# Transposing the row maxima of an attention batch: one matrix and four copies for four matrices and two copies

## The chip, the cores and the metric

One core of a Trainium2 chip runs the whole kernel. The metric is device time in microseconds (us) from start to end of one execution. The kernel before takes 259.82 us (median of three runs, 259.51 to 259.97).

## The reference, cut to what matters

Eight sequences of 128 tokens with 256 features go through a gated cross-attention (8 key heads of 8 features, 32 query heads, four of them to a key head) and then a gated mixture of 16 experts, of which each token uses two. The part around the change is the softmax of the attention:

```
q = (layernorm(x) @ Wq.T + bq);  k = ctx @ Wk.T + bk;  v = ctx @ Wv.T + bv
scores = einsum('bgrqd,bgkd->bgrqk', q, k) / sqrt(8)
scores = where(causal_mask, -inf, scores);  scores = where(padding_mask, -inf, scores)
w   = softmax(scores, axis=-1)
out = einsum('bgrqk,bgkd->bgrqd', w, v)          # then @ Wo.T + bo, gate, residual, experts
```

## The kernel before, in words

The kernel is written instruction by instruction: five programs, one for each engine, meet at semaphores, and the order on each engine is fixed by tables of slot numbers.

**What a batch does.** A batch is one of the eight sequences. Its scores are made twice by TensorE. `scores_q` computes them with queries on the partitions (128 queries by 4 key heads x 128 keys), in eight products (4 values of r, 2 halves hf of the heads); VectorE's `row_max` (L849) takes the negated maximum over the keys of each, so that `mneg` [128, R=4, G=8] holds 32 maxima for each query. `scores_k` computes the scores again, transposed, with keys on the partitions, in eight products (one for each key head g), which ScalarE's `Exp` (L668) turns into `pT`. The maximum must be subtracted per query, and queries then lie in the free dimension, so the subtraction is part of the product: the moving operand `q4` [128, 2, R, tokens] carries the three-part queries in its partitions 0 to 95 and the negated maxima in its partitions 96 to 111 (8 rows of high parts, 8 of low parts, `KR` = 3*QR + 2*G = 112), and the stationary operand `kz` has ones there for its head.

**The job MT** brings the maxima from `mneg` into these partitions. `max_parts` (L859 and L861, VectorE) writes their high and low parts into `mt`, at columns 96 to 111 of each of four matrices of 128 x 112, one for each r; the other columns are zero from a memset at the start (L470, GpSimd). TensorE transposes the four matrices (L1046), side by side into one PSUM bank, where the 16 wanted rows lie at partitions 96 to 111, 512 columns wide. ScalarE copies them to `q4`, once for each half of the heads (L588, L589: the two copies read the same 16 x 512 values), and the second copy raises `mt_ok`.

**The order of the work.** The main loop has 82 slots. In slot s < 64 TensorE issues `scores_k(s)` (L989: the mask product, listed in the trace as bank<-ident_b,cmask, then bank<-q,kz), then `scores_q` of 12 or so products ahead (bank<-kz,q, then bank<-cmask,ident_b), in slots with s % 8 == 5 and 0 the products with the values (bank<-pT,vz), and then the jobs of the slot. MT of batch b stands in slot 8b - 3, MT of batch 0 ahead of the loop. ScalarE takes a job's result one slot later, before the `Exp` of that slot: the copies of MT, b stand ahead of `Exp(8b - 2)`. `scores_k(n)` waits for `p_done` n - 1, that is for `Exp(n - 2)`, whose bank it writes; and for the first head of a batch, `scores_k(8b)`, also for `mt_ok` of its batch. So `scores_k(8b)` is the first product of TensorE that waits for what stands behind MT on ScalarE. Other jobs are TO, AT, WO, YT (output of attention: transposes, the product with Wo, the next transpose), SC, SN, CT and CB (router and expert weights). After slot 63 come the experts, all products of TensorE with VectorE and ScalarE behind it.

Of the kernel before, what the change touches and what calls it, by code (L numbers as in the profile page):

```python
# [92 lines left out]
def build(nc, x, ctx_in, m_qk, m_pad, g_x, g_f, Wq, bq, Wk, bk, Wv, bv, Wo, bo, Rw, Gw, Uw, Dw, consts, pick, out):  # L93
    es = ExitStack()
    with es:
# [54 lines left out]
        rstd = sb("rstd", [P, NB])  # L150
        nmr = sb("nmr", [P, NB])
        mneg = sb("mneg", [P, R, G])
        mt = sb("mt", [P, R, KR], F32R)
        pT = sb("pT", [P, 2, G // 2, R * L])
        o_sb = sb("o_sb", [P, R * L])
        rden = sb("rden", [P, R, G])
# [184 lines left out]
        def toks(t):  # L341
            return slice(t * L, (t + 1) * L)
# [214 lines left out]
        def _(sc):  # L557
# [4 lines left out]
            def high(j):  # L562

                sc.wait_ge(job_done, jn[j] + 1)
                ps, k = jbank(j), j[0]
                if k == "wkv":
                    ins = nc.scalar.copy(wkv[0], ps[:, 0:NKW].rearrange("p (c n) -> p c n", c=DC))
                elif k == "wq":
                    for c in range(DC):
                        ins = nc.scalar.copy(wq[0][:, c].rearrange("p (r g d) -> p r g d", r=R, g=G),  # L570
                                             ps[:, c * D:(c + 1) * D].rearrange("p (g r d) -> p r g d", g=G, r=R))
                elif k == "wo":
                    ins = nc.scalar.copy(wo[0][:], ps[:].rearrange("p (c n) -> p c n", c=DC))
                elif k in ("c", "x"):
                    ins = nc.scalar.copy((cT if k == "c" else xT)[0][:, j[2], half(j[1])], ps[:])
                elif k == "kv":
                    for hf in range(2):
                        ins = nc.scalar.activation(k4[0:QR, hf, half(j[1])], ps[QR * hf:QR * (hf + 1), :],
                                                   ACT.Identity, bias=bias[QR * hf:QR * (hf + 1), 2 * R + hf:2 * R + hf + 1])
                        if hf == 0:  # L580
                            ins.then_inc(job_hi, 1)
                elif k == "q":
                    ins = nc.scalar.activation(qc_hi[1][:, j[2]], ps[:], ACT.Identity,
                                               bias=bias[:, 2 * R + 3 + j[2]:2 * R + 4 + j[2]])
                elif k == "MT":
                    rows = slice(3 * QR, KR)
                    src = ps[rows, :].rearrange("p (r q) -> p r q", r=R)
                    nc.scalar.copy(q4[rows, 0, :, toks(j[1])], src)  # L588
                    nc.scalar.copy(q4[rows, 1, :, toks(j[1])], src).then_inc(mt_ok, 1)  # L589
                    return  # L590
                elif k == "AT":
                    if j[1]:
                        sc.wait_ge(job_done, jn["WO", j[1] - 1] + 1)
                    ins = nc.scalar.copy(aT[0][:], ps[:, 0:D].rearrange("p (c q) -> p c q", c=DC))
                elif k == "YT":
                    ins = nc.scalar.copy(xT[0][:, :, toks(j[1])], ps[:, 0:D].rearrange("p (c q) -> p c q", c=DC))
                ins.then_inc(job_hi, 1)
# [90 lines left out]
        def _(ve):  # L688
# [163 lines left out]
            def max_parts(b):  # L852

                ve.wait_ge(max_ok, G * (b + 1))
                if b:
                    ve.wait_ge(job_done, jn["MT", b - 1] + 1)
                else:
                    ve.wait_ge(pool_init, 3)
                own(nc.vector.tensor_copy(mt[:, :, 3 * QR:3 * QR + G], mneg[:]))  # L859
                settle()  # L860
                nc.vector.tensor_tensor(mt[:, :, 3 * QR + G:KR], mneg[:], mt[:, :, 3 * QR:3 * QR + G].bitcast(F32), ALU.subtract).then_inc(m_parts, 1)  # L861


            def best_two(h):
# [122 lines left out]
        def _(pe):  # L987
# [12 lines left out]
            def job(j):  # L1000
# [13 lines left out]
                elif k in ("wq", "wo"):  # L1014
                    src = wq_n if k == "wq" else wo_n
                    pe.wait_ge(d_wq if k == "wq" else d_wo, 16)
                    for c in range(DC):
                        for o in range(DC):
                            ins = nc.tensor.transpose(ps[:, c * D + o * P:c * D + (o + 1) * P],
                                                      src[:, o, c * P:(c + 1) * P], ident)  # L1020
                elif k in ("c", "x"):
                    _, h, c = j
                    if k == "c":
                        pe.wait_ge(d_ctx, 16 * (h + 1))
                    else:
                        pe.wait_ge(xn_ok, 1 + TPH * h)
                    src = c_sb if k == "c" else xn
                    for t in range(TPH):
                        ins = nc.tensor.transpose(ps[:, toks(t)], src[:, h * TPH + t, c * P:(c + 1) * P], ident)  # L1029
                elif k == "vn":  # L1030
                    pe.wait_ge(v_ok, j[1] + 1)
                    for b in range(TPH):
                        ins = nc.tensor.transpose(ps[:, b * 64:(b + 1) * 64], vT[64:128, toks(j[1] * TPH + b)],
                                                  ident[64:128, 64:128])
                elif k == "kv":
                    pe.wait_ge(*emptied(("c", j[1], 1)))
                    ins = three(ps[:], [lambda c, i=i: wkv[i][:, c] for i in range(2)],
                                [lambda c, i=i: cT[i][:, c, half(j[1])] for i in range(2)], DC)
                elif k == "q":
                    pe.wait_ge(*emptied(("x", j[1], 1)))  # L1040
                    ins = three(ps[:], [lambda c, i=i: wq[i][:, c, j[2] * P:(j[2] + 1) * P] for i in range(2)],
                                [lambda c, i=i: xT[i][:, c, half(j[1])] for i in range(2)], DC)
                elif k == "MT":
                    pe.wait_ge(m_parts, j[1] + 1)
                    for r in range(R):
                        ins = nc.tensor.transpose(ps[0:KR, r * L:(r + 1) * L], mt[:, r].bitcast(F32), ident)  # L1046
                elif k == "TO":
                    pe.wait_ge(o_ok, j[1] + 1)
                    for r in range(R):
                        ins = nc.tensor.transpose(ps[:, r * P:(r + 1) * P], o_sb[:, r * L:(r + 1) * L], ident)  # L1050
                elif k == "AT":
                    pe.wait_ge(*emptied(("TO", j[1])))
                    a = an[:].rearrange("p g r d -> p (g r d)")
                    for c in range(DC):
                        ins = nc.tensor.transpose(ps[:, c * L:(c + 1) * L], a[:, c * P:(c + 1) * P], ident)  # L1055
                elif k == "WO":
                    pe.wait_ge(*emptied(("AT", j[1])))
                    ins = three(ps[:, 0:D], [lambda c, i=i: aT[i][:, c] for i in range(2)],
                                [lambda c, i=i: wo[i][:, c] for i in range(2)], DC)
                elif k == "YT":  # L1060
                    pe.wait_ge(xn_ok, 1 + TPH + j[1] + 1)
                    for c in range(DC):
                        ins = nc.tensor.transpose(ps[:, c * L:(c + 1) * L], xn[:, j[1], c * P:(c + 1) * P], ident)  # L1063
                elif k == "SC":
                    pe.wait_ge(*emptied(("YT", (j[1] + 1) * TPH - 1)))
                    pe.wait_ge(rw_ok, 1)
                    ins = three(ps[:], [lambda c, i=i: rw[i][:, c] for i in range(2)],
                                [lambda c, i=i: xT[i][:, c, half(j[1])] for i in range(2)], DC)
                elif k == "SN":
                    pe.wait_ge(*emptied(("SC", j[1])))  # L1070
                    for t in range(TPH):
                        ins = nc.tensor.transpose(ps[:, t * E:(t + 1) * E], s16[0:E, toks(j[1] * TPH + t)], ident[0:E, 0:E])
                elif k == "CT":
                    pe.wait_ge(c2_ok, j[1] + 1)
                    for t in range(TPH):
                        ins = nc.tensor.transpose(ps[0:2 * E, toks(t)],
                                                  c2[:, j[1] * TPH + t].rearrange("p a e -> p (a e)").bitcast(F32), ident)
                elif k == "CB":
                    t, h = ORDER[j[1]]
                    pe.wait_ge(*emptied(("CT", h)))  # L1080
                    pe.wait_ge(pick_ok, 1)
                    ins = mm(ps[:], pick_r[:, t * P:(t + 1) * P], cwT[:, half(h)], True, True)
# [131 lines left out]
```

## Time and profile before

| | |
|---|---|
| median of three runs | 259.82 us |
| the profiled execution, its own time | 257.8 us |
| its span in the trace | 256.0 us |
| mean granted TensorE clock | 0.973 of full speed |
| TensorE busy with products | 228.1 us, 1243 instructions |
| VectorE busy | 174.8 us |
| ScalarE busy | 93.8 us |
| GpSimd busy | 98.3 us |

The first 19 us load and prepare, the attention's eight batches run to about 136 us, the experts from there to the end. PE is TensorE's products, PEld its weight loads, DVE VectorE, ACT ScalarE, POOL GpSimd. In the rows below a product's time is longer than its share of the engine, since products overlap; what one costs in a stream is read from the distance of the starts.

### The profile page before, as it was taken

The page shows a single profiled execution, that of the slowest core. Times are in us where ns is not written, and L with a number is a line of the kernel's source. Part 1 is how long each engine was busy: PE and PEld are TensorE (multiplying, and loading weights), DVE is VectorE, ACT ScalarE, POOL GpSimd, SP SyncE. Part 2 cuts the span into 40 slices and gives each one's busy share as a digit, 9 for nine tenths or more (in the row PEclk, how much of TensorE's full clock was granted, in tenths as well). Part 3 has the DMA queues.
Part 4 walks back from the last instruction along what each step waited for, and adds up shares of the span by engine and source line. Part 5 has one row for each costly group of instructions (what it writes and reads, how often), then busy time and mean ns, then how long its engine had stood idle before and what let it go on. Part 6 is the DMA issues. An engine that isn't in the chain of part 4 may idle for free.

```text
span 256.0 us, 3715 instructions
## 1 busy us (share of the span) xinstructions
PE 228.1 (89%) x1243; PEld 163.0 (64%) x1243; DVE 174.8 (68%) x358; ACT 93.8 (37%) x175; POOL 98.3 (38%) x131
## 2 busy tenths in 40 slices
PE   0679698999989999999588899799999999999993
PEld 0653364466545555555335787688888888888882
DVE  2659678658797677858921775698665766676565
ACT  2554248746656574747376221001010101011000
POOL 5355514400836193811711022229742563362000
PEclk9995589999999999999999999999999999999999
DMA  7571600007740002020020000003402220000004
GB/s 211 69 229 41 155 15 23 0 10 170 162 94 1 3 0 61 3 63 0 12 53 0 0 4 0 0 0 85 102 16 50 61 42 22 0 0 0 3 0 164
DMA packets 22418, 12.31 MB, mean 48 GB/s; under 512 B 14816, under 2 KB 21568, under 8 KB 22400
## 3 DMA queue, kind: packets, MB, share of 16 engines
q1 hardware_dynamic: 22096, 11.86, 19.4%
q10 hardware_dynamic: 304, 0.22, 0.4%
q8 instruction: 10, 0.16, 0.3%
q14 instruction: 8, 0.07, 0.1%
HBM read 7.91 MB, written 1.05 MB: 35 GB/s over the span
## 4 chain that ended last, share of the span: by engine, by line
PE 76%; DVE 13%; SPq 3%; DMA 3%; issue 2%; ACT 2%; DVEq 0%
PE bank L989 70%; DVE mneg L849 2%; DMA mqk_u<-in_mask_SxS_bc 2%; PE bank L1046 2%; PE bank L1050 2%; SPq L374 1%; PE bank L1029 1%; DVE x_sb L982 1%; DVE cb L895 1%; DMA q<-q 1%; DVE w L891 1%; PE bank L1055 1%; DVE xT L715 1%; DVE rw L953 1%; PE bank L1063 1%
## 5 line engine op out<-in xcount | busy, mean ns | idle before, releaser
L989 PE MATMUL bank<-xT,cT 128*128 128x512 f32 x288 | 70.5, 394 | 0.0
L989 PEld LDWEIGHTS bank<-xT,cT 128*128 128x128 f32 x288 | 53.7, 188 | 12.1 <-issue 0.8
L849 DVE TENSOR_REDUCE mneg<-bank 128x4 f32<-128x512 f32 x64 | 43.2, 685 | 13.8 <-PE bank L989 12.6
L668 ACT ACTIVATE pT<-bank 128x512 f32<-128x512 f32 x64 | 38.2, 599 | 23.6 <-PE bank L989 22.7
L655 ACT ACTIVATE pT<-bank 128x512 f32<-128x512 f32 x24 | 14.3, 597 | 81.1 <-PE bank L989 81.1
L989 PEld LDWEIGHTS bank<-w_d,q 128*128 128x128 f32 x288 | 37.4, 190 | 2.8 <-issue 1.3
L989 PE MATMUL bank<-w_d,q 128*128 128x256 f32 x288 | 38.3, 282 | 0.8 <-DVE q L927 0.8
L989 PE MATMUL bank<-q,kz 112*128 112x512 f32 x64 | 38.2, 598 | 0.0
L989 PE MATMUL bank<-kz,q 96*128 96x512 f32 x64 | 28.3, 452 | 3.3 <-DMA q<-q 1.9
L912 DVE TENSOR_TENSOR pT<-pT,bank 128x512 f32<-128x512 f32 x24 | 16.4, 683 | 18.5 <-PE bank L989 18.5
L921 DVE TENSOR_TENSOR pT<-pT,bank 128x512 f32<-128x512 f32 x24 | 16.5, 686 | 16.3 <-PE bank L989 16.0
L989 PE MATMUL bank<-cmask,ident_b 128*128 128x512 bf16 x64 | 26.4, 412 | 0.0
L989 PE MATMUL bank<-ident_b,cmask 128*128 128x512 bf16 x64 | 24.9, 389 | 1.2 <-ACT q L589 1.2
L453 POOL TENSOR_TENSOR vare<-mv,cst 128x1 f32<-128x1 f32 (+1 forms) x10 | 1.9, 194 | 60.7 <-DVE mv L703 53.4
L927 DVE TENSOR_TENSOR q<-pT,q 128x512 fp32r<-128x512 f32 x24 | 22.4, 933 | 0.8
L526 POOL TENSOR_TENSOR w_d<-padf,zero 128x256 fp32r<-128x256 f32 x12 | 7.4, 614 | 36.8 <-PE bank L989 36.5
L484 POOL TENSOR_TENSOR kz<-k,cst 112x512 fp32r<-112x512 f32 x16 | 16.3, 1043 | 11.1 <-DVE k L718 6.3
L523 POOL TENSOR_TENSOR cT<-c_sb,cT 128x512 fp32r<-128x512 f32 x12 | 18.1, 1509 | 0.9
L989 PEld LDWEIGHTS bank<-cmask,ident_b 128*128 128x128 bf16 x64 | 6.5, 101 | 17.9 <-issue 17.7
L989 PE MATMUL bank<-pT,vz 128*32 128x512 f32 x128 | 17.0, 605 | 0.7 <-ACT pT L668 0.7
L989 PEld LDWEIGHTS bank<-kz,q 96*128 96x128 f32 x64 | 13.0, 203 | 7.1 <-DVE mneg L849 3.3
L522 POOL TENSOR_TENSOR cT<-c_sb,zero 128x512 fp32r<-128x512 f32 x12 | 14.0, 1164 | 0.0
(131 smaller groups left out, 291.9 us busy)
## 6 DMA issues: line engine op xcount, KB each, us to landing
padf<-in_L_ffn_down_w SPq DMA_DIRECT2D x12, 128.0 KB, 2.3
c_sb<-in_ctx SPq DMA_DIRECT2D x2, 512.0 KB, 6.5
q<-cT SPq DMA_DIRECT2D x8, 128.0 KB, 2.7
out<-x_sb SPq DMA_DIRECT2D x4, 256.0 KB, 2.4
q<-xn SPq DMA_DIRECT2D x8, 96.0 KB, 2.2
c_sb<-in_L_ffn_gate_w SPq DMA_DIRECT2D x8, 96.0 KB, 2.1
c_sb<-in_L_ffn_up_w SPq DMA_DIRECT2D x8, 96.0 KB, 2.1
x_sb<-in_x SPq DMA_DIRECT2D x2, 256.0 KB, 3.6
```

Of the source, the lines that this page charges most:

```text
L484: ins = pool.tensor_tensor(kz[0:KR, s, g], k4[0:KR, hf, toks(b)].bitcast(F32).unsqueeze(1).to_broadcast([KR, GH, L]), cst[0:KR, C_G + GH * ...
L522: step(pool.tensor_tensor(w_gu[0][:, s], gu, zero[:].unsqueeze(2).unsqueeze(3).to_broadcast([P, 2, DC, P]), ALU.add))
L523: pool.tensor_tensor(w_gu[1][:, s], gu, w_gu[0][:, s].bitcast(F32), ALU.subtract).then_inc(w_ok, 1)
L526: step(pool.tensor_tensor(w_d[0][:, s], raw_d[:, s], zero[:].to_broadcast([P, D]), ALU.add))
L655: nc.scalar.activation(act_g[:, n % 2], bank[0][:], ACT.Silu).then_inc(a_ok, 1)
L668: nc.scalar.activation(pT[:, i // 4, i % 4, :], bank[2 + s % 2][:], ACT.Exp, scale=SCALE).then_inc(p_done, 1)
L849: nc.vector.tensor_reduce(mneg[:, r, 4 * hf:4 * hf + 4], bank[SQ_BANK[n % 3]][:].rearrange("p (g k) -> p g k", g=4), X, ALU.max, negate=Tr ...
L912: nc.vector.tensor_tensor(h_su[:, n % UL], act_g[:, n % 2], bank[1][:], ALU.mult).then_inc(u_free, 1)
L921: nc.vector.tensor_tensor(h_all, h_su[:, n % UL], jbank(j)[:], ALU.mult).then_inc(job_lo, 1)
L927: nc.vector.tensor_tensor(hl[:, n % 2], h_all, hh[:, n % 2].bitcast(F32), ALU.subtract).then_inc(h_ok, 1)
L989: return nc.tensor.matmul(dst, a, b, start=start, stop=stop, skip_group_check=True)
L1046: ins = nc.tensor.transpose(ps[0:KR, r * L:(r + 1) * L], mt[:, r].bitcast(F32), ident)
```

## The change

`mt` becomes one matrix of 128 x 128: for each r a block of 32 columns, of which the first 16 hold the high and low parts and the rest zeros. One transpose puts them all into the first 128 columns of the bank, the maxima of r at partitions 32r to 32r + 15. ScalarE then makes four copies, one for each r, each out of another quadrant of 32 partitions (32r), 16 partitions by 2 x 128 elements: the source is read twice (a stride of zero over the two halves of the heads), and the destination is partitions 96 to 111 of `q4`, both halves, that r. The last raises `mt_ok`. VectorE's two instructions write the same 32 values of a partition, at other columns.

```diff
-        mt = sb("mt", [P, R, KR], F32R)
+        mt = sb("mt", [P, R, P // R], F32R)
...
                 elif k == "MT":
-                    rows = slice(3 * QR, KR)
-                    src = ps[rows, :].rearrange("p (r q) -> p r q", r=R)
-                    nc.scalar.copy(q4[rows, 0, :, toks(j[1])], src)
-                    nc.scalar.copy(q4[rows, 1, :, toks(j[1])], src).then_inc(mt_ok, 1)
+                    for r in range(R):
+                        src = ps[r * P // R:r * P // R + 2 * G, 0:L].unsqueeze(1).to_broadcast([2 * G, 2, L])
+                        ins = nc.scalar.copy(q4[3 * QR:KR, :, r, toks(j[1])], src)
+                    ins.then_inc(mt_ok, 1)
                     return
...
-                own(nc.vector.tensor_copy(mt[:, :, 3 * QR:3 * QR + G], mneg[:]))
+                own(nc.vector.tensor_copy(mt[:, :, 0:G], mneg[:]))
                 settle()
-                nc.vector.tensor_tensor(mt[:, :, 3 * QR + G:KR], mneg[:], mt[:, :, 3 * QR:3 * QR + G].bitcast(F32), ALU.subtract).then_inc(m_parts, 1)
+                nc.vector.tensor_tensor(mt[:, :, G:2 * G], mneg[:], mt[:, :, 0:G].bitcast(F32), ALU.subtract).then_inc(m_parts, 1)
...
                 elif k == "MT":
                     pe.wait_ge(m_parts, j[1] + 1)
-                    for r in range(R):
-                        ins = nc.tensor.transpose(ps[0:KR, r * L:(r + 1) * L], mt[:, r].bitcast(F32), ident)
+                    ins = nc.tensor.transpose(ps[:, 0:L], mt[:].rearrange("p r m -> p (r m)").bitcast(F32), ident)
```

On TensorE, around MT of batch 2 (bank<-cst,mt is the transpose of `mt`, bank<-cst,an that of the job AT ahead of it; lines behind L1045 move up by one):

```order
 L989 MATMUL bank<-cmask,ident_b 128x512
 L989 MATMUL bank<-pT,vz 32x512 x4
-L1055 MATMUL bank<-cst,an 128x128 x2
-L1046 MATMUL bank<-cst,mt 112x128 x4
+L1054 MATMUL bank<-cst,an 128x128 x2
+L1045 MATMUL bank<-cst,mt 128x128
 L989 MATMUL bank<-ident_b,cmask 128x512
 L989 MATMUL bank<-q,kz 128x512
```

Four transposes have become one, in the same place; nothing else on TensorE moves, in this batch or in the others.

On ScalarE, at the same batch (q<-bank are the copies of the maxima, pT<-bank the exponentials, aT<-bank the job AT):

```order
 L668 ACTIVATE pT<-bank 128x512
 L594 CAST aT<-bank 128x256
-L588 CAST q<-bank 16x4x128
-L589 CAST q<-bank 16x4x128
+L588 CAST q<-bank 16x2x128 x4
 L668 ACTIVATE pT<-bank 128x512 x4
 L644 COPY o_sb<-bank 128x512
```

Two copies of 512 elements a partition have become four of 256, ahead of the same four exponentials.

## Rows read from the trace of the kernel before

**Rows 1.** The page: busy time, share of the span and instructions of each engine.
```profile
PE 228.1 (89%) x1243; PEld 163.0 (64%) x1243; DVE 174.8 (68%) x358; ACT 93.8 (37%) x175; POOL 98.3 (38%) x131
```

**Rows 2.** Windows: length, busy us (x) of PE, PEld, DVE, ACT, POOL, clock, DMA.
```profile
85.08:96.80 11.72, 11.72 (x71) 6.50 (x67) 8.25 (x16) 7.46 (x14) 7.47 (x11) 1.00 0.01 1
...
27.00:34.00 7.00, 4.76 (x17) 3.03 (x17) 3.60 (x10) 2.35 (x5) 4.61 (x5) 0.50 0.55 125
34.00:35.00 1.00, 1.00 (x8) 0.81 (x8) 0.91 (x2) 0.55 (x2) 0.00 (x0) 0.97 0.00 0
```

**Rows 3.** Timeline, batch 4: start, us, engine, line, operation, [idle before]; TensorE from MT on.
```profile
85.08 0.65 PE L1046 MATMUL bank<-cst,mt 128*112 128x128 f32 x4
85.57 0.38 PE L989 MATMUL bank<-ident_b,cmask 128*128 128x512 bf16 x1
...
88.13 0.38 PE L989 MATMUL bank<-ident_b,cmask 128*128 128x512 bf16 x1
```

**Rows 4.** Timeline, ScalarE, batch 4: the two copies, and the exponential behind them.
```profile
85.77 0.58 ACT L588 CAST q<-bank 16x512 fp32r<-16x512 f32 x1 [1.44 <-PE bank L1046]
...
86.86 0.60 ACT L668 ACTIVATE pT<-bank 128x512 f32<-128x512 f32 x1
```

**Rows 5.** The tile mt: TensorE's 32 transposes, ns least/median/most.
```profile
L1046 PE MATMUL bank<-cst,mt x32: 272/273/432, 28.1 to 122.5; 128*112 128x128 f32 x32
```

**Rows 6.** Timeline, TensorE: the two transposes of YT, and the product behind them.
```profile
81.74 0.38 PE L1063 MATMUL bank<-cst,xn 128*128 128x128 f32 x2
81.96 0.38 PE L989 MATMUL bank<-ident_b,cmask 128*128 128x512 bf16 x1
```

**Rows 7.** Timeline, batch 0: TensorE and ScalarE around the first MT.
```profile
28.09 1.07 PE L1046 MATMUL bank<-cst,mt 128*112 128x128 f32 x4 [1.31 <-DVE mt L861]
...
29.19 0.58 ACT L588 CAST q<-bank 16x512 fp32r<-16x512 f32 x1 [5.48 <-PE bank L1046]
29.68 0.57 ACT L589 CAST q<-bank 16x512 fp32r<-16x512 f32 x1
...
30.31 0.61 PE L989 MATMUL bank<-ident_b,cmask 128*128 128x512 bf16 x1 [1.15 <-ACT q L589]
```

**Rows 8.** Timeline, ScalarE: runs of two or eight instructions with nothing between them.
```profile
10.50 0.65 ACT L570 CAST w_t<-bank 128x256 fp32r<-128x256 f32 x2
...
15.89 3.06 ACT L610 ACTIVATE q<-bank,bias 32x128 fp32r<-32x128 f32 x8
...
39.15 1.39 ACT L578 ACTIVATE k<-bank,bias 32x512 fp32r<-32x512 f32 x2 [1.77 <-PE bank L989]
```

**Rows 9.** One line's instructions, L610: least, median and most ns.
```profile
L610 ACT ACTIVATE q<-bank,bias x8: 358/360/362, 15.9 to 18.6; 32x128 fp32r<-32x128 f32 x8
```

**Rows 10.** Timeline, batch 2: TensorE and ScalarE around MT.
```profile
60.18 0.60 PE L1046 MATMUL bank<-cst,mt 128*112 128x128 f32 x4
...
60.38 0.37 ACT L594 CAST aT<-bank 128x256 fp32r<-128x256 f32 x1 [1.20 <-PE bank L1055]
...
61.91 1.09 ACT L668 ACTIVATE pT<-bank 128x512 f32<-128x512 f32 x2
...
63.18 0.39 PE L989 MATMUL bank<-ident_b,cmask 128*128 128x512 bf16 x1
```

**Rows 11.** Timeline, batch 1: TensorE's MT and its `scores_k(8)`.
```profile
43.96 0.62 PE L1046 MATMUL bank<-cst,mt 128*112 128x128 f32 x4
...
47.16 0.38 PE L989 MATMUL bank<-ident_b,cmask 128*128 128x512 bf16 x1
```

**Rows 12.** Timeline, batch 7: MT, and TensorE's wait for the router's weights.
```profile
122.16 0.65 PE L1046 MATMUL bank<-cst,mt 128*112 128x128 f32 x4 [0.94 <-DVE xT L715]
...
126.76 0.60 PE L1076 MATMUL bank<-cst,c 128*32 128x128 f32 x4 [2.33 <-DVE c L901]
```

**Rows 13.** The chain of waits: the piece of VectorE that starts the way to it.
```profile
118.93 0.70 DVE mneg L849
```

**Rows 14.** Timeline, GpSimd: its first instruction behind the memsets of the start.
```profile
15.09 0.46 POOL L492 TENSOR_TENSOR cmask<-padf,mqk 128x128 bf16<-128x128 f32 x1 [6.55 <-DVE padf L836]
```

## The prediction
> **What bounds the kernel now.** I read the page first: TensorE is busy in 89% of the span, no other engine in more than 68% [rows 1]. An average hides stages, so I took one batch of the attention from one MT to the next by the view of windows [rows 2]: 11.72 us long, TensorE busy in all of them, VectorE in 8.25, ScalarE in 7.46, and the clock at full speed. There TensorE's stream of products is the bound, and what is taken out of it shortens the batch, as long as nobody else's wait fills the gap. The same view shows the granted clock at 0.50 from 27 to 34 us, the lower of the two levels (1.2 GHz), and at 0.97 from 34 to 35, nearly the upper (2.4 GHz). Then the timelines around each MT give what its transposes cost, when ScalarE's copies follow, and when TensorE next needs something that stands behind them.
>
> **TensorE, batches 1 to 6.** The products overlap, so the price is the distance of the starts. YT's two transposes start at 81.74 and the product behind them at 81.96: 0.22, or 0.11 each [rows 6]. MT's four take 0.49, from 85.08 to 85.57 [rows 3], a little over four times 0.11, since the first doesn't find its weights loaded; that part stays. Three fewer save 3 x 0.11 = 0.33 us in a batch, 6 x 0.33 = **1.98 us**. That each transpose now has 128 columns of weights and not 112 I cost at nothing: YT's have 128 already.
>
> **ScalarE's copies, their price.** A cast of 256 elements a partition takes 0.37 us [rows 10], one of 512 takes 0.58 [rows 4]. How closely can four follow? The two copies before start 0.49 apart though the first lasts 0.58: they overlap by 0.09 [rows 7]. The casts of L570 do as well: two in 0.65, so 0.65 - 0.37 = 0.28 apart [rows 8, 10]. But these pairs start in one and the same quadrant. L610 reads each of its eight instructions out of another quadrant than the one before (QR * i), and there 3.06 = 7 x 0.386 + 0.36: they start 0.386 apart and last 0.360 [rows 8, 9], with no overlap and a gap of 0.026. L578's two, from quadrants 0 and 1, take 1.39, again no overlap [rows 8]. The new copies are of that kind. So the interval is between 0.28 (overlap) and 0.60 (as long as the old ones, none); I take 0.37 + 0.026, about **0.39**, since L610 is the nearest row. The page "ScalarE: Activation LUTs" of the Trainium skill, section on what ACT_TABLE_LOAD costs, says that back-to-back ACTIVATEs overlap by about 93 ns, and makes no exception for quadrants. By that the copies would be 0.28 apart and the gain larger, the first rival below; the trace agrees where the quadrant stays, and disagrees at L610 and L578.
>
> **Does ScalarE make TensorE wait?** What stands behind the copies is `Exp(8b - 2)`, and `scores_k(8b)` waits for it and for `mt_ok`. In batch 4 the one transpose starts at 85.08 and lasts 0.27 [rows 3, 5]; before, the four ended at 85.73 and ScalarE started at 85.77 [rows 3, 4], 0.04 behind, so now it starts at 85.39. Four copies take 1.56, so the exponential starts at 86.95 (before 86.86) and ends 0.60 later, at 87.55. TensorE now comes to `scores_k(8b)` at 88.13 - 0.33 = 87.80 [rows 3]. A slack of 0.25 is left, about 0.2 with the semaphore: hidden, but narrowly; before it was 88.13 - 87.46 = 0.67. Batch 1: 43.96 + 0.31 + 1.56 + 0.60 = 46.43 against 47.16 - 0.33 = 46.83 [rows 11], hidden. Batches 3, 5 and 6 are built as batch 4. Batch 2 differs: ScalarE is at AT's cast from 60.38 to 60.75 and can only then start the copies, at 60.78; exponential at 62.34, end 62.94, and TensorE wants it at 63.18 - 0.33 = 62.85 [rows 10]. TensorE waits about 0.13, and a weight load of the mask may come uncovered: I take **0.2 us lost**, between 0 and 0.3.
>
> **Batch 0** stands ahead of the loop, at half clock, and all of it is on the path: DVE, four transposes, two copies, product [rows 7]. The transposes: 28.09 to 29.19 when ScalarE starts; one of them lasts 0.43 at this clock [rows 5], the longest of the 32, so ScalarE starts at 28.55, 0.64 earlier. The copies: 3 x 0.39 + 0.37 = 1.54 for 1.06, 0.48 longer. TensorE goes on 0.16 earlier. It then works at half speed until 34; if the clock rises at the same instant as before, half of that is lost again. I take **0.1**, between 0.08 and 0.16 (with overlap 0.49).
>
> **Batch 7**: nothing. MT at 122.16 is followed by a wait of 2.33 for the router's weights at 126.76 [rows 12], which VectorE makes in a chain that starts at 118.93 from a product of TensorE [rows 13]. The gains of the batches before move that start, this one's only lengthens the wait; the copies have that time too.
>
> **The rest.** GpSimd's memset of `mt` is shorter by 320 elements, and it idles 6.55 before its next work [rows 14]: nothing. VectorE's instructions keep their sizes, and at a stride of 32 elements instead of 112 I expect the same time; it idles 3.5 us of a batch [rows 2]. No DMA and no wait of another engine is moved; MT's bank comes free with `mt_ok`, two slots and more before the next job there.
>
> **Sum**: 1.98 - 0.2 + 0.1 + 0 = **1.9 us**. The profiled execution took 257.8 with a span of 256.0; it would take 255.9. It lies 2.0 below the median of the runs shown, a difference I can't place; the gain hangs on the attention's stretch at full clock, so I put it on the median: 259.8 - 1.9 = **257.9 us**.
>
> **Rivals.**
> 1. *The copies overlap in spite of the quadrants* (0.28 apart). Batch 2 doesn't wait, batch 0 gives 0.49 at the engine, about 0.35 at the end: 1.98 + 0.35 = 2.3, so 257.5. For it: a copy without a pointer operand is the simpler instruction, and L610 and L578 have one, in changing quadrants too. Against: nothing else distinguishes L610 from L570.
> 2. *Part of the gain is taken up on the way.* The slack of 0.2 in batches 3 to 6 is small. Copies 0.45 to 0.50 apart would make TensorE wait 0.05 to 0.25 in each of four batches and 0.4 to 0.6 in batch 2; or VectorE's maxima, which TensorE awaits in the early batches, don't shift with it. Gain about 1, 258.8.
> 3. *ScalarE becomes the bound behind each MT, and the kernel is slower.* The place is `scores_k(8b)`, the price the interval of the copies. At 0.60 the exponential of batch 4 ends at 85.39 + 2.40 + 0.60 = 88.39; TensorE waits 0.6 and loses 0.3 against before. Four such batches 1.2, batch 1 0.15, batch 2 0.64, batch 0 about 0.5: 2.5 slower, 262.3. It turns at about 0.52. For it: a source read twice through a stride of zero has no row of its own. Against: the elements written are counted in every row I have, and there are half as many.
> 4. *The clock rises later.* Before MT of batch 0 TensorE idles 1.31 and behind it 1.15 [rows 7]; now it does less and idles about 1.6 behind it, in the stretch at 0.50. Every us more at that level costs a busy engine half a us; 3.8 more would take all the gain, and the time would stay at 259.8. From 30.3 on TensorE is as busy as before, which speaks against it.
>
> That the change doesn't do what it says I exclude: both lists of instructions show one transpose and four casts at each of the eight places.
>
> **How the numbers follow.** A measurement of this kernel can tell 0.2%, 0.5 us, from no change. Forecast (gain 1.4 to 2.2) 0.55; rival 1 (2.2 to 2.9) 0.13; rival 2 (0.5 to 1.4) 0.17; rival 4 or another near zero 0.08; rival 3 0.07. Faster 0.85, same 0.08, slower 0.07. The range takes in the first three and the upper edge of the fourth: 256.9 to 259.3.
>
> **What would show it.** The copies' interval behind MT: 0.39 confirms the quadrants, 0.28 rival 1, over 0.45 rivals 2 or 3. MT to the next product 0.16 instead of 0.49. The window from MT to MT 11.4 instead of 11.72. ScalarE as releaser of `scores_k(16)`, once, with 0.1 to 0.2; the same at 24, 32, 40 and 48 would be rival 2. TensorE's start behind the first copies at 30.15, and the clock up at 34. The wait before CT 2.3 plus 0.3 at most. Wrong would be a batch that stays at 11.7.

## The result, and the profile after

The changed kernel takes 256.42 us (median of four, 256.26 to 258.50), the kernel before 259.89 in the same rounds; the ratio is 0.990, 95% interval 0.986 to 0.994. Twelve more executions gave 256.56, ratio 0.991 (0.988 to 0.994). So the changed kernel is faster, by about 1%, 1.5 to 3.8 us; the medians say 3.3 to 3.5, the ratio 2.4 to 2.6, the two profiled executions 257.8 - 256.26 = 1.5. Why these three differ is the larger part of what follows. Forecast was a gain of 1.9, in a range of times from 256.9 to 259.3, and the median of 256.42 lies 0.5 below that range.

The page of the profile after: busy time, instructions, and the clock in 40 slices.

```profile
PE 225.4 (89%) x1219; PEld 160.6 (63%) x1219; DVE 174.5 (69%) x358; ACT 97.0 (38%) x191; POOL 98.0 (39%) x131
...
PEclk9999589999999999999889999999999999999999
```

TensorE has 24 products fewer and 2.7 us less busy time, ScalarE 16 instructions and 3.2 us more [rows 1]. The clock row shows two dips, one near 30 us, which the first profile of before has too, and one near 126 us, which it doesn't have.

The windows of the profile after: batch 4 from MT to MT, and two stretches for the clock (the last three columns are granted clock, DMA share and GB/s).

```profile
83.52:94.91 11.39, 11.39 (x67) 6.20 (x64) 8.24 (x16) 7.83 (x16) 7.45 (x11) 1.00 0.00 0
126.00:131.00 5.00, 4.62 (x24) 2.07 (x17) 0.78 (x2) 2.82 (x6) 0.46 (x3) 0.71 0.19 49
32.00:36.00 4.00, 4.00 (x20) 2.54 (x18) 2.66 (x6) 2.27 (x4) 0.98 (x2) 0.84 0.11 23
```

The batch takes 11.39 for 11.72 [rows 2]: 0.33, as the sum had it, TensorE still busy in all of it. TensorE and ScalarE in this batch (start, us, engine and line, as in the rows of before):

```profile
83.52 0.33 PE L1045 MATMUL bank<-cst,mt 128*128 128x128 f32 x1
83.69 0.38 PE L989 MATMUL bank<-ident_b,cmask 128*128 128x512 bf16 x1
...
86.25 0.38 PE L989 MATMUL bank<-ident_b,cmask 128*128 128x512 bf16 x1
...
83.89 1.49 ACT L588 CAST q<-bank 16x256 fp32r<-16x256 f32 x4 [1.12 <-PE bank L1045]
85.41 1.17 ACT L668 ACTIVATE pT<-bank 128x512 f32<-128x512 f32 x2
```

MT takes 0.17 of TensorE's stream instead of 0.49 [rows 3]. The four copies take 1.49: at 0.364 each, (1.49 - 0.364) / 3 = 0.375 apart, no overlap. The exponential starts 1.89 behind MT (before 1.78 [rows 3, 4]) and ends at 85.41 + 0.60 = 86.01, 0.24 ahead of `scores_k(32)` at 86.25. Batch 2, where ScalarE is late:

```profile
59.29 0.27 PE L1045 MATMUL bank<-cst,mt 128*128 128x128 f32 x1
...
62.06 0.39 PE L989 MATMUL bank<-ident_b,cmask 128*128 128x512 bf16 x1
...
61.40 1.09 ACT L668 ACTIVATE pT<-bank 128x512 f32<-128x512 f32 x2
```

From MT to `scores_k(16)` it is 2.77, before 3.00 [rows 10]: 0.23 gained, 0.10 spent on the wait. But that 0.10 comes back before the batch is over. MT of batch 3 waits for VectorE in both kernels, 1.07 after and 1.19 before, and starts 72.21 - 59.29 = 12.92 behind MT of batch 2, before 73.45 - 60.18 = 13.27: the batch gains 0.35, as much as the others. The two MT of batch 3, after and then before:

```profile
72.21 0.33 PE L1045 MATMUL bank<-cst,mt 128*128 128x128 f32 x1 [1.07 <-DVE xT L715]
```

```profile
73.45 0.65 PE L1046 MATMUL bank<-cst,mt 128*112 128x128 f32 x4 [1.19 <-DVE xT L715]
```

Batch 0 and the wait for the router's weights:

```profile
27.80 0.45 PE L1045 MATMUL bank<-cst,mt 128*128 128x128 f32 x1 [1.59 <-DVE mt L861]
29.83 0.61 PE L989 MATMUL bank<-ident_b,cmask 128*128 128x512 bf16 x1 [1.58 <-ACT q L588]
...
124.21 0.60 PE L1075 MATMUL bank<-cst,c 128*32 128x128 f32 x4 [2.64 <-DVE c L901]
```

From MT to the next product 2.03 for 2.22 [rows 7]; the wait before CT 2.64 for 2.33 [rows 12]. In all, the profile after is 2.55 us ahead of the profile before when CT starts (124.21 for 126.76), and only 1.5 ahead at the end. Of the 2.55, 0.29 are there before MT of batch 0 starts (27.80 for 28.09), before the change has touched TensorE or ScalarE; such an offset stands between profiles of one program up to there too (27.68 and 28.03 in after_fill0 and after_fill2). The missing 1.0 us lies right behind CT, where the clock stands at 0.50.

### The profile page after: what moved, and what is told of

It reads as the page before. It is cut to its first block, busy times and chain, and to the rows that moved or that the text cites. A ratio compares the mean times of both kernels' runs of the same rounds, so it can differ in the third digit from the quotient of the medians.

```text
span 254.5 us, 3683 instructions
## 1 busy us (share of the span) xinstructions
PE 225.4 (89%) x1219; PEld 160.6 (63%) x1219; DVE 174.5 (69%) x358; ACT 97.0 (38%) x191; POOL 98.0 (39%) x131
## 4 chain that ended last, share of the span: by engine, by line
PE 79%; DVE 13%; DMA 3%; issue 2%; ACT 2%; ACTq 0%; DVEq 0%
PE bank L989 71%; DVE mneg L849 3%; PE bank L1029 2%; DMA wkv_n<-in_L_xattn_Wv 2%; PE bank L1049 2%; DVE x_sb L982 1%; DVE cb L895 1%; DMA q<-q 1%; PE bank L1045 1%; DVE w L891 1%; PE bank L1054 1%; ACT q L588 1%; DVE xT L715 1%; DVE rw L953 1%; PE bank L1062 1%
## 5 line engine op out<-in xcount | busy, mean ns | idle before, releaser
L989 PEld LDWEIGHTS bank<-w_d,q 128*128 128x128 f32 x288 | 37.4, 190 | 2.8 <-issue 1.3
L989 PE MATMUL bank<-q,kz 112*128 112x512 f32 x64 | 39.0, 611 | 0.0
L989 PE MATMUL bank<-kz,q 96*128 96x512 f32 x64 | 26.6, 425 | 4.8 <-DVE mneg L849 3.2
L989 PE MATMUL bank<-cmask,ident_b 128*128 128x512 bf16 x64 | 25.0, 391 | 0.0
L989 PE MATMUL bank<-pT,vz 128*32 128x512 f32 x128 | 17.7, 626 | 0.7 <-ACT pT L668 0.7
L989 PEld LDWEIGHTS bank<-kz,q 96*128 96x128 f32 x64 | 12.4, 194 | 8.5 <-DVE mneg L849 4.7
L588 ACT CAST q<-bank 16x256 fp32r<-16x256 f32 x32 | 11.6, 364 | 12.1 <-PE bank L1045 11.8
```

What stands on the lines that cost most here:

```text
L588: ins = nc.scalar.copy(q4[3 * QR:KR, :, r, toks(j[1])], src)
L989: return nc.tensor.matmul(dst, a, b, start=start, stop=stop, skip_group_check=True)
```

## The experiments

A table first, of all fourteen profiled executions, since each has pieces that can be set side by side. Times in us; "stretch" is from MT of batch 1 to CT of the first half, "behind" from there to CT of the second half, and "start" from the product behind MT of batch 0 to MT of batch 1, each from the chain of waits and the timeline of that profile. The clock is the granted one of two windows. The last four rows are of kernels with fillers or with CT moved, which come further down.

| kernel | time | start | stretch | behind | clock 32 to 36 | 126 to 131 |
|---|---|---|---|---|---|---|
| before, first profile | 257.80 | 13.65 | 82.80 | 36.40 | 0.74 | 1.00 |
| before_look_a | 259.87 | 14.04 | 82.90 | 37.84 | 0.63 | 0.66 |
| before_look_b | 257.54 | 13.44 | 82.84 | 36.40 | 0.81 | 1.00 |
| three_back | 258.40 | 13.61 | 82.71 | 36.39 | 0.66 | 1.00 |
| before_fill2 | 256.76 | 13.68 | 82.64 | 36.42 | 1.00 | 1.00 |
| changed, first profile | 256.26 | 13.55 | 80.83 | 37.42 | 0.84 | 0.71 |
| after_again | 256.07 | 14.40 | 80.81 | 36.34 | 0.59 | 1.00 |
| one_quadrant | 258.52 | 15.57 | 80.85 | 37.85 | 0.50 | 0.68 |
| after_fill2 | 255.23 | 13.59 | 80.72 | 36.35 | 1.00 | 1.00 |
| six_copies | 259.72 | 14.66 | 82.53 | 37.68 | 0.50 | 0.73 |
| before_fill0 | 260.32 | 15.33 | 82.88 | 37.61 | 0.69 | 0.81 |
| after_fill0 | 259.03 | 16.01 | 80.90 | 37.92 | 0.77 | 0.66 |
| ct_later | 253.57 | 13.51 | 80.91 | 34.74 | 0.85 | 1.00 |
| ct_later_fill0 | 254.13 | 13.68 | 80.89 | 34.68 | 1.00 | 1.00 |

The stretch is the same within 0.3 in all six profiles with four transposes, and within 0.2 in the seven with one transpose and four copies, 2.0 apart. Most of what varies between executions of a kernel is in the two other columns, and it goes roughly with the clock beside it: "behind" is 36.3 to 36.4 where the clock stays up and 37.4 to 37.9 where it falls, as long as CT is in its old slot. The windows are fixed, so a fall that reaches past one is shown in part only (both kernels with the first fillers).

### The changed kernel again

No edit.

> The changed kernel, unchanged, for more executions and the granted clock of each. Theory A (three transposes fewer in each of six batches, 0.33 us each, plus some tenths at batch 0; what else differs between executions is TensorE's clock, which falls at other places): MT to the next product 0.11 to 0.17, four copies 0.375 apart, 2.0 to 2.8 us faster than before in the median. Rival B (the gain of 3.5 us in the medians is all the change's): 3.3 to 3.6 faster again, and executions of the same clock as before's show it too.

Measured: 256.56 us median of 12 (255.58 to 258.92) beside 259.81 of before (257.61 to 260.53, 29 executions), ratio 0.991 (0.988 to 0.994). Copies 0.375 apart, MT 0.16 of the stream. By the medians it is rival B's 3.3. But the executions of both kernels fall into groups: of before, 6 of 29 lie under 258.5 and 22 over 259.3; of the changed kernel, 9 of 12 under 257.0 and 3 over 258.2. The lower groups are some 1.3 us apart, the upper ones 1.2; the median compares the upper group of the one with the lower of the other. So B's number came, but not by its reason; what the change is worth at the same clock, the pieces of the table and the fillers below tell. That the lower groups are 1.3 apart and not 2.0 fits the table: both profiles of the changed kernel are from its lower group, and each pays at one of the two places (37.42 behind CT in the first, 14.40 in the start in after_again), while before_look_b, from the lower group of before, pays at neither.

### Three transposes put back

```diff
-                    ins = nc.tensor.transpose(ps[:, 0:L], mt[:].rearrange("p r m -> p (r m)").bitcast(F32), ident)
+                    for r in range(R - 1, -1, -1):
+                        ins = nc.tensor.transpose(ps[:, r * L:(r + 1) * L], mt[:].rearrange("p r m -> p (r m)").bitcast(F32), ident)
```

> One part undone: TensorE transposes the one matrix four times (the first three into columns that nobody reads), ScalarE keeps its four copies. Theory A: six batches give back 0.33 us each and batch 0 about 0.3 to 0.6, so 2.3 to 2.6 slower than the changed kernel and about as slow as before or up to 0.5 us slower. Rival C (the gain comes from the later or shorter work of ScalarE or from GpSimd's shorter memset): stays within 0.5 us of the changed kernel.

Measured: 260.35 us median of 12 (258.40 to 261.46), 3.8 over the changed kernel, more than expected; ratio to before 1.004 (1.002 to 1.007). Profile beside profile it is 258.40 - 256.07 = 2.3, the expected size, 1.9 of it in the stretch (82.71 for 80.81); at batch 0 it is 2.66 from MT to the next product for 2.02, the 0.6 of the expectation's upper end. The rest of the 3.8 is again which group the executions fall into: one of 12 under 259. The gain is TensorE's three transposes, and rival C falls: with ScalarE's four copies and the shorter memset kept, it is gone.

### All four copies out of one quadrant

```diff
-                        src = ps[r * P // R:r * P // R + 2 * G, 0:L].unsqueeze(1).to_broadcast([2 * G, 2, L])
+                        src = ps[0:2 * G, 0:L].unsqueeze(1).to_broadcast([2 * G, 2, L])
```

> All four copies read partitions 0 to 15, the maxima of r = 0, so the other heads get the wrong maxima subtracted; every instruction keeps its size. Theory D (a copy that starts in another quadrant than the one ahead of it isn't overlapped): copies 0.28 apart for 0.375, the exponential behind them 0.3 to 0.4 earlier, batch 0 0.3 faster, the whole 0.1 to 0.5 us faster. Rival E (the interval belongs to small copies or to the stride of zero): still 0.375 apart, time the same.

The timeline of ScalarE in batch 4:

```profile
85.67 1.15 ACT L588 CAST q<-bank 16x256 fp32r<-16x256 f32 x4 [1.12 <-PE bank L1045]
86.84 0.60 ACT L668 ACTIVATE pT<-bank 128x512 f32<-128x512 f32 x1
```

The same four copies take 1.15 for 1.49: (1.15 - 0.364) / 3 = 0.26 apart for 0.375. Size, stride of zero and destination are unchanged, only the start partition of the source is another; so rival E falls, and a change of the source's quadrant costs 0.11 us for each copy. That it is the change and not quadrant 0 itself, six_copies shows below, where pairs out of one quadrant overlap in the second and fourth quadrants too. The page "ScalarE: Activation LUTs" of the Trainium skill, section on what ACT_TABLE_LOAD costs, has the overlap of back-to-back ACTIVATEs, about 93 ns, without that condition; these rows agree with it only where the quadrant stays (0.364 - 0.262 = 0.10 us). The same source quadrant isn't enough for every pair. The exponential reads from quadrant 0 as well, and it starts at 86.84, 0.02 behind the end of the fourth copy; elsewhere in this profile a cast and the exponential behind it do overlap, 0.25 apart:

```profile
119.34 0.37 ACT L594 CAST aT<-bank 128x256 fp32r<-128x256 f32 x1
119.59 0.62 ACT L668 ACTIVATE pT<-bank 128x512 f32<-128x512 f32 x1
```

There both also write from partition 0 on, while the copies write from partition 96. That the quadrant of the destination counts too would fit, but no run varied it.

Batch 0 goes on 1.69 behind MT for 2.03, 0.34 earlier, as expected. The stretch stays at 80.85: ScalarE's time was hidden there. Time 255.68 median of 5 (255.61 to 258.52), 0.9 under the changed kernel's, where 0.1 to 0.5 was expected; the pieces show only the 0.34 of batch 0, and where the rest lies stays open, since the profiled one is the slowest of the five, its clock at 0.50 until beyond 36 us and again behind CT: it pays 15.57 in the start and 37.85 behind.

### Two copies more

```diff
+        scr = sb("scr", [P, NB, R, 2, L], U8)
...
                     for r in range(R):
                         src = ps[r * P // R:r * P // R + 2 * G, 0:L].unsqueeze(1).to_broadcast([2 * G, 2, L])
+                        if r % 2:
+                            nc.scalar.copy(scr[3 * QR:KR, j[1], r], src)
```

> Two copies more for each MT, of the same size and sources, to a scratch tile: the suspected cost of ScalarE raised by half. Theory F (the slack at the first product of a batch is about 0.2 us, beyond it each us on ScalarE is a us of TensorE): exponential 0.75 later behind MT, TensorE waits about 0.5 in each of batches 3 to 6, 0.3 in batch 1, 0.8 in batch 2, 0.4 to 0.75 in batch 0: 3 to 4 us slower than the changed kernel, slower than before by about 1. Rival G (ScalarE has room enough): within 1 us of the changed kernel, only batch 0's 0.75 shows.

Measured: 260.05 us median of 10 (259.65 to 260.56), 3.5 over the changed kernel, ratio to before 1.003 (1.000 to 1.005). TensorE's timeline at `scores_k(32)`, and then one line of its waits between 30 and 135 us (in total, times, longest):

```profile
88.77 0.39 PE L992 MATMUL bank<-ident_b,cmask 128*128 128x512 bf16 x1 [0.17 <-ACT pT L671]
```

```profile
PE bank L992 <- ACT pT L671: 1.3, 6, 0.5
```

A wait on ScalarE has appeared in six places. (A copy to the scratch tile and the one behind it share their source's quadrant and overlap, 0.27 apart, so the two add 0.52, not 0.75.) In batch 4 the exponential starts 2.41 behind MT for 1.89, 0.52 later, and `scores_k(32)` 3.06 for 2.73, 0.33 later: 0.19 of the 0.52 was free. That is the slack of 0.24 less 0.05 from the exponential's end to TensorE's start. Theory F's mechanism holds, and the change spent 0.43 of the 0.67 there was. The stretch is 82.53 for 80.81, 1.7 longer: with half a microsecond more per batch on ScalarE nearly the whole gain of the change is gone. In batch 2 TensorE waits longest, 0.49, and nothing of it is left at MT of batch 3, which now waits 0.48 for VectorE and not 1.07. The waits of 1.3 in all are less than half of what was expected, and that the total came out at 3 to 4 is in part luck: against after_again, 1.3 of the 3.65 between the two profiles lie behind CT, where this execution's clock falls.

### TensorE kept busy in its first idle times, in both kernels

```diff
+            def fill(dst, times):
+                for _ in range(times):
+                    mm(dst[:].rearrange("p (r q) -> p r q", r=R), ident_b[:], ident_b[:].unsqueeze(1).to_broadcast([P, R, L]), True, True)
+
+            pe.wait_ge(*emptied(("bias",)))
+            fill(bank[2], 7)
             for n in range(G):
                 scores_q(n)
+                if 3 <= n < G - 1:
+                    fill(bank[2], 2)
+            fill(bank[2], 6)
             job(("MT", 0))
+            fill(bank[2], 5)
```

> The changed kernel with TensorE's idle time of the first 30 us filled: 7 products nobody reads ahead of the first scores, 2 behind each of four of them, 6 ahead of MT of batch 0 and 5 behind it, 0.22 us each at full clock. Theory H (the executions fall into two groups, near 256.4 and near 258.7, by when the granted clock rises behind batch 0; idle time there lets it fall): clock at 1.00 from 20 to 36 us, one group only, median 254.5 to 255.5. Rival I (the groups come from elsewhere): clock up, time 1 us less at most and still two groups 2 us apart.

> The kernel before with the same fillers. Theory H: one group, 3 us or more below its median of 259.8, and 2.2 to 2.6 above the changed kernel with fillers, which is the price of the change without the clock (six batches of 0.33 and 0.2 to 0.6 at batch 0). Rival B (3.3 us are the change's own): 3.3 above the changed kernel with fillers.

Measured: the changed kernel 257.83 us (255.19 to 259.75, 6 executions), before 258.70 (256.86 to 261.58, 12). A miss for Theory H as it was put: before gained 1.1, not 3, the changed kernel lost 1.3, and both spread more than without fillers. The 257.83 is the middle of a gap, with three executions up to 256.64 and three from 259.03, so the two medians say little. Sorted by the mean clock of the execution, the two kernels agree with Theory A: at 0.997 or more the changed kernel has 255.19 and before 256.86 to 257.48 (5 executions). What sets the slower ones back, the profile of after_fill0 shows (windows, then TensorE's timeline):

```profile
34.00:36.00 2.00, 2.00 (x8) 1.55 (x8) 1.02 (x2) 0.41 (x1) 0.00 (x0) 0.54 0.00 0
36.00:38.00 2.00, 2.00 (x7) 0.81 (x7) 1.37 (x3) 0.77 (x2) 0.00 (x0) 0.61 0.00 0
126.00:130.00 4.00, 3.54 (x16) 1.16 (x16) 1.96 (x6) 0.60 (x1) 1.16 (x4) 0.57 0.43 92
```

```profile
33.78 0.47 PE L989 MATMUL bank<-kz,q 96*128 96x512 f32 x1 [2.20 <-DMA q<-qc_lo]
```

With its clock at full, TensorE arrives early at the first scores of batch 1 and waits 2.20 us for the transfers of the queries, which SyncE issues one behind another (twelve between 23.56 and 32.03 us); behind that wait the clock falls, and the busiest part of the start runs at 0.54 and 0.61. The idle time was moved, not removed. The profile shows one more thing: of the idle time around MT of batch 0 little is to be had while that queue ends last.

### The same, and the wait for the router's weights filled

```diff
+                    for _ in range(10 if j[1] == 0 else 0):
+                        mm(ps[:].rearrange("p (r q) -> p r q", r=R), ident_b[:], ident_b[:].unsqueeze(1).to_broadcast([P, R, L]), True, True)
                     pe.wait_ge(c2_ok, j[1] + 1)
```

> As after_fill0, and ten more such products in the wait of 2.6 us for the router's weights (job CT of the first half), where the profile of the changed kernel shows the clock at 0.50 for 3.5 us behind the wait. Theory H: clock 1.00 all through, 1.1 us less than after_fill0 in those executions that have that fall; median 253.8 to 254.5, the fastest of all. Rival J (the fall behind CT is rare or harmless): the same as after_fill0 within 0.3.

> The kernel before with both kinds of fillers: the clean comparison. Theory A: 2.2 to 2.6 us above after_fill2, each with a spread under 0.5 us. Rival B: 3.3 or more above it.

Measured: 255.47 us (255.08 to 257.28, 6 executions) and 257.81 (256.76 to 261.67, 12). Expected were 253.8 to 254.5 for the changed kernel, which is missed by 1 us, and a spread under 0.5 us for each, missed as well. But the two profiles have a clock of 1.00 in every window. Windows and timeline of before_fill2:

```profile
20.00:36.00 16.00, 13.39 (x62) 6.42 (x61) 12.67 (x28) 5.72 (x11) 7.25 (x7) 1.00 0.36 83
36.00:131.00 95.00, 90.64 (x506) 50.79 (x505) 70.61 (x156) 57.33 (x107) 40.36 (x63) 1.00 0.20 44
```

```profile
32.86 0.47 PE L989 MATMUL bank<-kz,q 96*128 96x512 f32 x1 [1.46 <-DMA q<-qc_lo]
```

And of after_fill2:

```profile
20.00:36.00 16.00, 13.08 (x59) 6.07 (x59) 12.66 (x27) 6.38 (x13) 7.41 (x7) 1.00 0.36 84
36.00:131.00 95.00, 90.51 (x499) 49.39 (x497) 71.31 (x158) 61.36 (x125) 40.26 (x63) 1.00 0.19 44
```

```profile
33.31 0.47 PE L989 MATMUL bank<-kz,q 96*128 96x512 f32 x1 [1.35 <-DMA q<-qc_lo]
```

This is the clean comparison: 82.64 for 80.72 in the stretch, 1.92 us, and nothing at batch 0, since both end there in the same wait for the transfers, 5.27 and 5.28 behind MT. (The two profiled times are only 1.5 apart, because this profile of before is 0.44 ahead already at MT of batch 0, 27.59 for 28.03.) Among the executions of these two kernels whose mean clock is 0.997 or more, before has 256.76 to 258.08 (8, middle 257.25) and the changed kernel 255.08 to 255.60 (4, middle 255.28): 2.0 apart. Theory A holds, rival B falls. Rival J falls too: "behind" is 36.35 here and 37.42 in the changed kernel's first profile.

### Two more profiles of the kernel before

> The kernel before, unchanged: a profile of another execution. Theory K (its executions near 259.9 are those whose granted clock rises later behind batch 0, about 37 us instead of 34, and falls once more behind the wait for the router's weights): if its time is near 259.9, windows show 0.50 beyond 34 us or at 126 to 130 us, and the pieces between them take the same time as in the first profile. If it is near 257.8, one or both are missing. Rival L: near 259.9 with the clock as in the first profile, the 2 us in other pieces.

> As before_look_a: one more profile of the kernel before, to see a second execution's clock beside its time.

By luck one came from each group: 259.87 and 257.54. Windows, first before_look_a, then before_look_b:

```profile
32.00:36.00 4.00, 4.00 (x18) 2.82 (x17) 2.21 (x5) 1.81 (x5) 1.36 (x2) 0.63 0.11 26
36.00:124.00 88.00, 84.45 (x469) 47.90 (x469) 66.44 (x146) 53.32 (x101) 36.54 (x56) 1.00 0.19 43
...
126.00:131.00 5.00, 3.65 (x16) 1.29 (x16) 2.82 (x8) 0.60 (x1) 1.88 (x5) 0.66 0.36 80
```

```profile
32.00:36.00 4.00, 4.00 (x20) 2.70 (x19) 2.66 (x7) 2.27 (x4) 1.17 (x2) 0.81 0.13 30
...
126.00:131.00 5.00, 3.70 (x24) 1.84 (x24) 1.90 (x6) 2.46 (x5) 1.16 (x4) 1.00 0.37 84
```

Both stand at 0.50 from 28 to 32 us. At a mean of 0.63 over the next four microseconds the clock stood at the lower level for (1 - 0.63) x 2 x 4 = 3.0 of them, to 35.0; at 0.81 for 1.5, to 33.5. And in the execution of 259.87 it fell behind the wait before CT for (1 - 0.66) x 2 x 5 = 3.4 us, in the other not. The pieces: start 0.60 and behind 1.44 longer, stretch equal; 2.0 of the 2.3. Theory K holds, but for the 37 us that I had expected for the rise. Not every low stretch costs: in the first profile of before the clock is at 0.50 from 21 us on, in look_b only from 27 on, and the product behind MT of batch 0 starts at 30.31 and 30.23. So the mean clock of an execution alone doesn't tell its group. The page "TensorE: Matmul & The Clock Gate" of the Trainium skill, section on the clock gate, says that its window runs freely and isn't tied to the kernel's start, so that the instant of a change varies; the traces are in keeping with it, 33.5 and 35.0 in two executions of one program, but no run here separates that from small differences in what TensorE did before.

### The router's transposes two slots later

```diff
-        ROUTE = {"SC": (48, 73), "SN": (49, 75), "best": (51, 76), "weights": (53, 77), "CT": (55, 78)}
+        ROUTE = {"SC": (48, 73), "SN": (49, 75), "best": (51, 76), "weights": (53, 77), "CT": (57, 78)}
```

> The changed kernel with the transposes of the router's weights (job CT of the first half) in slot 57 instead of 55. Theory M (TensorE's wait of 2.6 us there is mostly avoidable, and with it the clock's fall behind it): the wait is gone or under 1 us, part of it comes back at the next job that needs VectorE (TO or YT of batch 6); 1 to 2.5 us faster than the changed kernel, 254 to 255.5 in the median, no clock at 0.50 between 120 and 135 us. Rival N (VectorE is the bound there, whatever TensorE does): the wait moves to the next job as a whole, under 0.5 us gained.

> The same with the idle time of the first 30 us filled as in after_fill0: the fastest version if Theories H and M both hold, 253 to 254.5, with the clock at 1.00 except where a filler falls short. If H's gain is taken by the transfers of the spread queries, which TensorE awaits at 33 us once its clock is full, then not faster than ct_later by more than 0.5.

Measured: 254.82 us (253.57 to 255.50, 6 executions), ratio to before 0.981 (0.977 to 0.986); with the first fillers 254.00 (253.65 to 255.98), ratio 0.980 (0.975 to 0.984). TensorE's waits between 110 and 130 us (in total, times, longest), after_again and then ct_later:

```profile
PE bank L1075 <- DVE c L901: 2.6, 1, 2.6
PE bank L1045 <- DVE xT L715: 0.9, 1, 0.9
PE bank L1049 <- ACT o_sb L644: 0.8, 1, 0.8
```

```profile
PE bank L1045 <- DVE xT L715: 0.9, 1, 0.9
PE bank L1062 <- ACT xn L649: 0.8, 1, 0.8
PE bank L989 <- ACT pT L668: 0.6, 1, 0.6
PE bank L1049 <- ACT o_sb L644: 0.3, 1, 0.3
```

The wait of 2.6 is gone, 0.9 of it is back in smaller ones: from MT of batch 6 to CT of the second half it takes 52.67 for 54.26, 1.6 less, with the clock at 1.00 behind CT in both, and no window from 124 to 131 us is under 1.00. Theory M holds. Its one line, beside the change, beats both kernels, 1.7 in the medians below the changed one. The fillers on top make 0.8 in the medians of six executions each, more than the 0.5 expected if the transfers took it all; their fastest execution is no faster.

## Why the prediction was right, and where not

- **The bound and the main term: right.** 0.33 us in each of six batches, 1.98. Measured: 11.39 for 11.72 from MT to MT, 1.9 to 2.0 in the stretch in the pairs of profiles, and three_back gives it back.
- **The copies' price: right.** 0.39 apart forecast, 0.375 measured; one_quadrant shows that L610 was the row to take, and rival 1 (0.28) is what it would be without the change of quadrants.
- **Batch 2's wait: forecast as a loss of 0.2, and nothing was lost.** The wait came, 0.1 long, but MT of batch 3 waits for VectorE anyway, and that wait was shorter by the same 0.1: the whole 1.98 arrived. The sum followed ScalarE's delay to `scores_k(16)` and not on to TensorE's next wait. The slack elsewhere: 0.25 forecast, 0.24 measured. Rival 3, slower through ScalarE, was real and near: half a microsecond more per batch, as six_copies shows, and the gain in the loop is all but gone.
- **Batch 0: right, 0.16 forecast, 0.19 measured** at the product behind the copies; the clock then takes its part, and with the fillers, where TensorE waits for the transfers behind it, nothing is left of it.
- **Batch 7: right as far as its own time goes.** The wait grew from 2.33 to 2.64 and took it up.
- **The step that failed is the last, from the gain to the time: "a difference I can't place ... so I put it on the median".** The measured median is 256.4, below the range, whose lower end allowed a gain of 2.9; the medians moved by 3.3 to 3.5. The profiled execution of before lay 2.0 under its median because it had no fall of the clock behind CT and an early rise behind batch 0, and most executions have both worse. I treated the clock as one rival with one place (batch 0) and one sign. It has two places, together worth 2.0 us between the two later profiles of before, as much as the change; and the changed kernel was in its lower group more often (9 of 12; before 6 of 29 in the same rounds, 7 of 23 and 2 of 11 in the later ones, at 258.6 and less). That is where 257.9 became 256.4. The time of 257.9 with a gain of 1.9 would have been right only if both kernels had spread over their groups alike.
- **Open:** why the changed kernel falls into the lower group more often. It starts TensorE's work behind batch 0 some tenths earlier (29.83 and 29.91 for 30.23 to 30.41), and three_back and six_copies, which start it at 31.05 and 30.22, are nearly always in the upper group; one_quadrant, at 29.58, is in the lower one in four of five. That fits, but no run varied that instant alone, and its profiled execution has the latest rise of all.

## What to carry to other kernels

Price an instruction in a stream by the distance of its neighbours' starts, and look in the same trace for a pair that has the feature you add (here the change of quadrant) before you believe in an overlap. Where engines change places, write down the slack at the first instruction that waits: it was 0.67 us, the change spent 0.43, and two copies more spent nearly the whole gain. Follow a delay past the first wait, too: where the next wait is for another engine, the delay can vanish in it. And where a core idles for one or two microseconds again and again, compare executions piece by piece with the granted clock beside each, not medians alone.

## What the runs showed of the hardware

- Two of these copies overlap on ScalarE by some 0.1 us if their sources start in the same quadrant of partitions, and not at all if they don't: 0.26 to 0.27 apart against 0.375, same sizes (one_quadrant, six_copies).
- Reading a PSUM source twice through a stride of zero costs no more than reading as many elements: 0.364 us for 16x256, 0.37 for 128x256.
- An idle time of 2.3 to 2.6 us of TensorE at one place was followed by a fall of the granted clock to 0.50 in some executions of a program and not in others (1.0 to 1.6 us each time). In the profiled executions of the two kernels with the first fillers alone, the clock stayed up to the next wait, fell behind that one, and fell again behind CT.
